# A two-layer cross-attention kernel with expert feed-forwards: gates spread by fp32r matmuls instead of through memory, and the second layer's first keys and queries loaded another way

## The chip, the core and the metric

The kernel runs on one core of a Trainium2 chip. The core has a matmul engine (TensorE, PE in the profile; PEld is its weight loads), a vector engine (DVE), a scalar engine (ACT), GpSimd (POOL) and SyncE (SP), which here issues nearly all DMAs. The engines run their own instruction streams and wait for each other by semaphores. The metric is the device time of one execution in microseconds (us). Before the change it is 2705.45 us, the median of three runs (2705.42 to 2705.73).

## The reference

Two layers work on x (1024 rows, 128 channels) against a context of 6404 rows. Each layer is a 16-head cross-attention (8 channels a head) and a feed-forward with 8 experts of which each row uses two, both added to x through a tanh gate.

```
def _L1_ffn_ref(x, W1, b1, W2, b2, Wr, br):
    logits = xf @ Wr + br
    topk_val, topk_idx = jax.lax.top_k(logits, K)          # K = 2 of 8 experts
    scores = jax.nn.softmax(topk_val, axis=-1)
    h = jnp.einsum('nd,edh->enh', xf, W1) + b1[:, None, :]
    a, g = jnp.split(h, 2, axis=-1)
    act = jax.nn.silu(a) * g
    out_e = jnp.einsum('enh,ehd->end', act, W2) + b2[:, None, :]
...
x = x + jnp.tanh(g_xattn[0]) * _L0_xattn_ref(_layernorm(x, axis=-1), ctx_1024, ctx_1024, ...)
x = x + jnp.tanh(g_ffn[0]) * _L0_ffn_ref(_layernorm(x, axis=-1), ...)
x = x + jnp.tanh(g_xattn[1]) * _L1_xattn_ref(ctx_1024, ctx_1024, _layernorm(x, axis=-1), mask, ...)
x = x + jnp.tanh(g_ffn[1]) * _L1_ffn_ref(_layernorm(x, axis=-1), ...)
```

Layer 0's experts have 512 hidden channels and a gelu; layer 1's have 256 hidden channels, a silu and a second product. The kernel computes all eight experts for all rows and multiplies each expert's hidden values by the row's gate, which is zero for the six experts that were not chosen.

## The kernel before

**Attention.** Keys and queries are projected for all heads at once, split into a high fp32r part and the remaining low part (`split_keys`, `queries`, L620), and stored to memory as `k_parts` and `q_parts` (`store_k` L255, `store_q` L261). For each head SP loads the 8 rows of that head back in the layout that the score matmuls need: `load_keys` (L297) issues 16 DMAs a head into one of the two slots of `k_ring`, and `load_queries` (L306) issues 4 into one of the three slots of `q_ring`. Each slot holds both parts twice, for two halves of the rows of x (partition rows 0 and 64). For each head PE first computes all scores once for the maxima (L947), DVE reduces them (L657), then PE computes them again (L928), ACT takes the exponentials (L495), and PE weighs the values (L976). The first head's maxima (`FIRST_UNITS`, 52 units of one L947 pair and one L657) stand alone at the start of each attention; later maxima are interleaved with the scores.

**Feed-forward.** `top_two` on DVE computes the gates `ga[:, 4]` (last instruction L782). PE turns them (`turn_gates`, L1056), ACT copies them out as `gate_t`, 8 partitions of 1024 (`gates_turned`, L518). Every engine below needs the gate of an expert on all 128 partitions. So `spread_gates` on SP (L351, L354) stores `gate_t` to memory as `gate_rows` and loads each of the eight rows back, broadcast to 128 partitions, as `gate_bc`, which lies in `k_ring`. `experts` on PE walks 16 units u = 0 to 15 (expert u // 2, half u % 2): `up(u)` is four matmuls (L1074), `down(u - 1)` is four in layer 0 and two in layer 1 (L1082). ACT applies gelu or silu (L528, L540). DVE multiplies the hidden values by the gate (L792 in layer 0; L805 and then L811 in layer 1), and `down` waits for that product.

**The hand-over between the layers.** Since `gate_bc` has overwritten `k_ring`, POOL must write the rows of ones again (`set_ring(1)`, L402, two memsets) after the last gate product of layer 0. SP, whose DMAs are issued in program order, then does `load_first(1)`: keys of head 0, the stores of the new queries (`store_q`), queries of heads 0 and 1, keys of head 1, queries of head 2. Meanwhile DVE, ACT and PE compute the layer norm and the queries of layer 1 (L604 to L620, L897, L905). PE's first maximum of layer 1 waits for the keys and the queries of head 0; ahead of it PE, DVE and SP each branch on a flag (L1122, L826, L276) between a masked and an unmasked program.

**The start.** SP stores the queries and the keys of layer 0, then does `load_first(0)`, and then loads the mask in ten pieces (`check_mask`, L267), which ACT sums (L467) in turn with its copies of the values (L440).

## Time and profile before

| What | us |
|---|---|
| median of three runs | 2705.45 |
| the profiled execution, its own time | 2710.2 |
| its span | 2708.1 |
| PE busy, DVE busy, ACT busy | 2494.6, 2161.4, 1939.4 |
| mean granted clock of PE | 0.941 |
| hidden-layer stages: layer 0, layer 1 (start of the gates to the last `down`) | about 1289 to 1416, 2598 to 2700 |
| hand-over between the layers, last `down` to the first maximum of layer 1 | about 1416 to 1466 |

The span is the profiled execution from the first to the last instruction; 2.1 us of its time lie outside the span, and the execution was 4.75 us above the median. The times in the rows below are microseconds from the start of the span. A granted clock of 1.00 is TensorE's level of 2.4 GHz, 0.50 its level of 1.2 GHz.

### The profile page before, as it was taken

How to read it: one execution, taken by the hardware profiler on the slowest of the kernel's cores; microseconds unless marked ns; L12 is line 12 of the kernel's file. 1: busy time of each engine (PE TensorE's matmuls, PEld its weight loads, DVE VectorE, ACT ScalarE, POOL GpSimd, SP SyncE). 2: the span in 40 equal slices, each digit the busy share in tenths (PEclk: the TensorE clock that was granted, in tenths of full speed). 3: DMA queues.
4: the chain of work that ended last, by engine and by line, in shares of the span. 5: the costliest groups of instructions: out<-in, count | busy, mean ns of one | idle time of the engine just before them, and what ended most of it. 6: DMA issues, size and time to landing. Idle time of an engine off the chain costs nothing.

```text
span 2708.1 us, 51412 instructions
## 1 busy us (share of the span) xinstructions
PE 2494.6 (92%) x21338; PEld 967.9 (36%) x21340; DVE 2161.4 (80%) x2211; ACT 1939.4 (72%) x3545; POOL 41.2 (2%) x28
## 2 busy tenths in 40 slices
PE   2389999999999999997893899999999999999979
PEld 1243333333333333343441333333333333333334
DVE  5468999999999999944434899999999999999234
ACT  2058888888888888874330188888888888888932
POOL 4000000000000000000010000000000000000000
PEclk8559999999999999999895699999999999999989
DMA  7120000000000000003101000000000000000010
GB/s 251 68 78 23 29 29 29 27 28 28 29 29 29 28 28 28 20 32 113 63 0 61 11 27 28 29 29 29 29 28 28 28 29 29 29 29 14 2 63 8
DMA packets 38612, 102.86 MB, mean 38 GB/s; under 512 B 4164, under 2 KB 14936, under 8 KB 38120
## 3 DMA queue, kind: packets, MB, share of 16 engines
q1 hardware_dynamic: 36936, 99.14, 10.0%
q8 instruction: 170, 2.79, 0.4%
q10 hardware_dynamic: 1440, 0.40, 0.1%
q14 instruction: 66, 0.54, 0.1%
HBM read 83.72 MB, written 15.80 MB: 37 GB/s over the span
## 4 chain that ended last, share of the span: by engine, by line
PE 64%; DVE 29%; SPq 3%; DMA 3%; issue 1%; ACT 1%; POOL 1%; ACTq 0%; DVEq 0%; POOLq 0%
DVE m_part L657 26%; PE ps L976 23%; PE ps L928 19%; PE ps L947 10%; PE ps L1074 4%; PE ps L1082 3%; SPq L297 2%; PE ps L888 1%; DMA q_parts<-probs 1%; PE ps L918 1%; SPq L306 1%; DMA probs<-in_mask_t 1%; PE ps L880 1%; PE ps L995 1%; DVE probs L613 1%
## 5 line engine op out<-in xcount | busy, mean ns | idle before, releaser
L657 DVE TENSOR_REDUCE m_part<-ps 128x2 f32<-128x1024 f32 (+1 forms) x1664 | 1933.7, 1184 | 209.0 <-PE ps L947 199.7
L495 ACT ACTIVATE probs<-ps 128x512 f32<-128x512 f32 (+1 forms) x3264 | 1763.8, 595 | 325.2 <-PE ps L928 213.6
L976 PE MATMUL ps<-probs,v_all 128*9 128x256 f32 x13056 | 1014.2, 383 | 1.7 <-ACT o_raw L475 0.5
L928 PE MATMUL ps<-q_ring,k_ring 35*128 35x512 f32 x3264 | 871.1, 498 | 0.6 <-ACT q_ring L484 0.4
L947 PE MATMUL ps<-k_ring,q_ring 33*128 33x512 f32 (+1 forms) x3328 | 733.7, 420 | 94.6 <-DVE m_part L657 36.2
L928 PEld LDWEIGHTS ps<-q_ring,k_ring 35*128 35x128 f32 x3264 | 349.5, 183 | 697.2 <-ACT probs L495 603.3
L947 PEld LDWEIGHTS ps<-k_ring,q_ring 33*128 33x128 f32 x3328 | 350.9, 194 | 183.2 <-DVE m_part L657 110.1
L976 PEld LDWEIGHTS ps<-probs,v_all 128*9 128x9 f32 x13056 | 195.3, 89 | 551.4 <-ACT probs L495 466.0
L792 DVE TENSOR_TENSOR probs<-probs,k_ring 128x512 f32<-128x512 f32 x64 | 43.6, 691 | 64.9 <-ACT probs L528 56.6
L678 DVE RECIPROCAL r_den<-ps 128x8 f32<-128x8 f32 x32 | 6.6, 207 | 110.6 <-PE ps L955 110.6
L482 ACT ACTIVATE q_ring<-ps 3x512 fp32r<-3x512 f32 x32 | 18.8, 587 | 102.2 <-PE ps L918 101.5
L528 ACT ACTIVATE probs<-ps,b_col 128x512 f32<-128x512 f32 x64 | 43.7, 687 | 65.5 <-PE ps L1074 58.5
L888 PE MATMUL ps<-w_att,ctx_t 128*128 128x128 f32 (+1 forms) x204 | 40.2, 358 | 31.7 <-ACT v_all L440 31.7
L467 ACT ACTIVATE probs<-probs 128x2560 bf16<-128x2560 uint16 (+1 forms) x11 | 23.9, 2177 | 60.2 <-DMA probs<-in_mask_t 60.1
L540 ACT ACTIVATE probs<-ps,b_col 128x512 f32<-128x512 f32 x32 | 20.2, 683 | 65.2 <-PE ps L1074 65.2
L1074 PE MATMUL ps<-big,ctx_t 128*128 128x512 f32 x128 | 61.3, 622 | 5.8 <-DVE probs L805 5.8
L1082 PE MATMUL ps<-probs,big 128*128 128x512 f32 x128 | 59.2, 608 | 4.5 <-DVE probs L792 4.5
L897 PE MATMUL ps<-ident_f,probs 128*128 128x128 f32 x32 | 8.8, 450 | 56.1 <-DVE probs L613 40.2
L1074 PE MATMUL ps<-big 128*128 128x512 f32 x128 | 59.2, 606 | 0.0
L402 POOL MEMSET k_ring<- 32x13056 f32 (+1 forms) x4 | 35.8, 8944 | 1381.9 <-DVE probs L792 1381.8
L805 DVE SCALAR_TENSOR_TENSOR probs<-ps,b_col,probs 128x512 f32<-128x512 f32 x32 | 23.9, 748 | 35.3 <-PE ps L1074 35.3
L888 PEld LDWEIGHTS ps<-w_att,ctx_t 128*128 128x128 f32 (+1 forms) x204 | 35.7, 256 | 43.4 <-ACT v_all L440 32.7
(122 smaller groups left out, 598.3 us busy)
## 6 DMA issues: line engine op xcount, KB each, us to landing
k_ring<-k_parts SPq DMA_DIRECT2D x384, 96.0 KB
k_ring<-k_parts SPq DMA_DIRECT2D x128, 112.2 KB
k_ring<-gate_rows SPq DMA_DIRECT2D x16, 512.0 KB, 7.3
probs<-in_mask_t SPq DMA_DIRECT2D x10, 640.0 KB, 4.4
k_parts<-probs SPq DMA_DIRECT2D x12, 512.0 KB, 3.1
k_parts<-big SPq DMA_DIRECT2D x12, 512.0 KB, 3.1
q_ring<-q_parts SPq DMA_DIRECT2D x128, 32.0 KB
big<-in_w SPq DMA_DIRECT2D x1, 2048.0 KB, 10.7
```

What stands on the lines that cost most here:

```text
L297: sp.dma_start(k_ring[row:row + PARTS * HD, off + k0:off + k1].bitcast(F32), of.broadcast_to([PARTS, HD, k1 - k0])).then_inc(key_in(l, h, ...
L402: nc.gpsimd.memset(k_ring[row:row + 32, 0:wide].bitcast(F32), 1.0).then_inc(sem("ring_set"), 1)
L495: A(probs[0:k, n % PSLOTS, HALF * half:HALF * half + HALF], ps[0:k, e_bank(unit), :], ACT.Exp, scale=SCALE).then_inc(sem(f"exp_done{l}"), 1)
L528: A(h_ring[:, u % 4, :], ps[:, u % 4, :], ACT.Gelu_apprx_tanh, bias=b1_col[:, 0, e * 4 + t:e * 4 + t + 1]).then_inc(sem("act_done0"), 1)
L657: V.tensor_reduce(m_part[:, h % 2, :, p, c], mx(n % 2)[:, :, 0:chunk_w[c]], AX.X, ALU.max).then_inc(sem(f"mx_done{l}"), 1)
L792: V.tensor_tensor(hg_ring[:, u % 8, :], h_ring[:, u % 4, :], gate_bc[:, e, HALF * half:HALF * half + HALF], ALU.mult).then_inc(sem("gated0 ...
L888: mm = pe.matmul(ps[0:width(t), bank + c % banks, P * (t % 4):P * (t % 4) + P], ctx_t[:, P * t:P * t + width(t)], w_att[:, l, 2, :], start ...
L928: pe.matmul(bank, k_ring[row:row + ROWS_EXP, koff:koff + P], q_ring[row:row + ROWS_EXP, qoff:qoff + HALF], start=not masked, stop=True).th ...
L947: mm = pe.matmul(bank[:, 0:w], q_ring[row:row + ROWS_MAX, qoff:qoff + P], k_ring[row:row + ROWS_MAX, koff:koff + w], start=not masked, sto ...
L976: mm = pe.matmul(ps[32 * g:32 * g + VW, 7, 0:QGW], v_all[:, t, h, :], probs[:, n % PSLOTS, QGW * g:QGW * g + QGW], start=(t == 0), stop=(t ...
L1074: pe.matmul(ps[:, t, :], w1[:, e, P * t:P * t + P], x_t[:, HALF * half:HALF * half + HALF], start=True, stop=True).then_inc(sem(f"hidden{l ...
L1082: mm = pe.matmul(ps[:, 4 + half, :], w2[:, e, t, :], hg_ring[:, n % 8, :], start=(e == 0 and t == 0), stop=False)
```

## The change

Three things change.

1. The gates no longer go through memory. DVE splits them into a high fp32r part and the rest (`gate_hl`, two instructions more), PE turns 16 rows in place of 8, ACT copies them to `gate_t`, which now lies in rows 0 to 15 of `q_ring`. For each unit u a matmul `spread(u)` with the constant `pick_e` (16 rows, each column repeated 128 times) writes the gate of the unit's expert and half, on all 128 partitions, to PSUM bank 6 or 7. DVE's products L792 and L811 (now L794 and L813) read the gate from there. The final matmul with b2 has 16 rows.
2. `k_ring` is not overwritten by gates, so the second pair of memsets on POOL is gone, and SP loads the keys of heads 0 and 1 of layer 1 as soon as they are stored and the last two heads of layer 0 are scored.
3. The first head's queries are copied from `q_st` straight into `q_ring`, by eight DMAs of 8 partitions each, ahead of the stores of the queries, in both layers. In layer 0 these now come before the stores of the keys.

```diff
-        gate_rows = [nc.dram_tensor(f"gate_rows{l}", [E, TQ], F32, kind="Internal").ap() for l in range(2)]
...
-        gate_bc = k_ring[:, 0:E * TQ].bitcast(F32).rearrange("p (e q) -> p e q", e=E)
...
                 for of in (flat3(probs)[:, 2 * TQ:], spare)]
-        gate_t = spare[0:E, KST * PARTS * HALF:KST * PARTS * HALF + TQ]
...
-        b2_sb = sb("b2_sb", [E, 2, C])
+        b2_sb = sb("b2_sb", [2 * E, 2, C])
+        pick_e = sb("pick_e", [2 * E, E], F32R)
...
+        gate_hl = spare[:, ga_at + 6 * QT * E + 6 * QT:ga_at + 8 * QT * E + 6 * QT].rearrange("p (t e) -> p t e", t=QT)
...
                                      ).then_inc(query_in(l, h)[0], 16)
-            def ready(l, what):
-
-                if what == "q":
-                    sp.wait_ge(sem(f"q_stored{l}"), 16 * 2)
-                else:
-                    for n in range(KST):
-                        sp.wait_ge(sem(f"k_stored{l}_{n}"), 16 * len(range(n, NCH, KST)))
-
-            def load_first(l):
-
-                sp.wait_ge(sem("ring_set"), RING_SET[l])
-                ready(l, "k")
-                if l:
+            def keys_stored(l):
+                for n in range(KST):
+                    sp.wait_ge(sem(f"k_stored{l}_{n}"), 16 * len(range(n, NCH, KST)))
+
+            def first_queries(l):
+
+                for half in range(2):
+                    sp.wait_ge(sem(f"q_split{l}"), half + 1)
+                    for b in range(PARTS):
+                        for part in range(PARTS):
+                            row = HB * half + (b * PARTS + part) * HD
+                            sp.dma_start(q_ring[row:row + HD, 0:HALF].bitcast(F32), q_st[0:HD, half, part, :].bitcast(F32)
+                                         ).then_inc(query_in(l, 0)[0], 16)
+                store_q(l)
+
+            def load_first0():
+
+                sp.wait_ge(sem("ring_set"), RING_SET)
+                first_queries(0)
+                store_k(0)
+                keys_stored(0)
+                for g in range(len(K_GROUPS)):
+                    load_keys(0, 0, g)
+                sp.wait_ge(sem("q_stored0"), 16 * 2)
+                load_queries(0, 1)
+                for g in range(len(K_GROUPS)):
+                    load_keys(0, 1, g)
+                load_queries(0, 2)
+
+            def load_first1():
+
+                keys_stored(1)
+                for h in range(KRING):
+                    sp.wait_ge(sem("scored0"), SCORE_AT["score", H - KRING + h, 2 * NT - 1] + 1)
                     for g in range(len(K_GROUPS)):
-                        load_keys(l, 0, g)
-                    store_q(l)
-                ready(l, "q")
-                load_queries(l, 0)
-                if l == 0:
-                    for g in range(len(K_GROUPS)):
-                        load_keys(l, 0, g)
-                load_queries(l, 1)
-                for g in range(len(K_GROUPS)):
-                    load_keys(l, 1, g)
-                load_queries(l, 2)
+                        load_keys(1, h, g)
+                first_queries(1)
+                sp.wait_ge(sem("q_stored1"), 16 * 2)
+                load_queries(1, 1)
+                load_queries(1, 2)
             def load_heads(l):
...
-            def spread_gates(l):
-                sp.wait_ge(sem(f"gate_t{l}"), 1)
-                sp.dma_start(gate_rows[l], gate_t[:, :]).then_inc(sem(f"gate_out{l}"), 16)
-                sp.wait_ge(sem(f"gate_out{l}"), 16)
-                for e in range(E):
-                    sp.dma_start(gate_bc[:, e, :], gate_rows[l][e:e + 1, :].rearrange("e q -> (e q)").partition_broadcast(P)
-                                 ).then_inc(sem(f"gate_bc_{e}"), 16)
-
...
             sp.dma_start(w2_1.rearrange("p e t d -> p (e t) d"),
                          a["w2_1"].rearrange("e (t f) d -> f (e t) d", f=P)).then_inc(sem("experts_in1"), 16)
-            spread_gates(0)
-            load_first(1)
+            load_first1()
             build_mask()
             load_heads(1)
-            spread_gates(1)
             sp.wait_ge(sem("x_final"), 1)
             sp.dma_start(out.rearrange("(t p) c -> p t c", p=P), x_sb[:, :, :]).then_inc(sem("out_stored"), 16)
...
+                nc.gpsimd.tensor_tensor(pick_e[:, :], ident_f[0:2 * E, 0:E], ident_f[0:2 * E, E:2 * E], ALU.add).then_inc(sem("pick_e"), 1)
...
-            set_ring(1)
...
-                A(gate_t[:, :], flat(ps[0:E, 6:8, :]), ACT.Identity).then_inc(sem(f"gate_t{l}"), 1)
+                A(gate_t[:, :], flat(ps[0:2 * E, 6:8, :]), ACT.Identity).then_inc(sem(f"gate_t{l}"), 1)
...
-                V.tensor_tensor(gate, tmp, spread(1), ALU.mult).then_inc(sem(f"gates{l}"), 1)
+                link(V.tensor_tensor(gate, tmp, spread(1), ALU.mult))
+                link(V.tensor_copy(gate_hl[:, :, 0:E].bitcast(F32R), gate))
+                V.tensor_tensor(gate_hl[:, :, E:2 * E], gate, gate_hl[:, :, 0:E], ALU.subtract).then_inc(sem(f"gates{l}"), 1)
             def gate_experts0():
                 for u in range(E * 2 * 4):
-                    e, half = u // 8, (u // 4) % 2
+                    half = (u // 4) % 2
                     dve.wait_ge(sem("act_done0"), u + 1)
-                    if u % 8 == 0:
-                        dve.wait_ge(sem(f"gate_bc_{e}"), 16)
+                    if u % 4 == 0:
+                        dve.wait_ge(sem("gate_spread0"), u // 4 + 1)
                     if u >= 8:
                         dve.wait_ge(sem("down0"), u - 7)
-                    V.tensor_tensor(hg_ring[:, u % 8, :], h_ring[:, u % 4, :], gate_bc[:, e, HALF * half:HALF * half + HALF],
+                    V.tensor_tensor(hg_ring[:, u % 8, :], h_ring[:, u % 4, :], ps[:, 6 + half, :],
                                     ALU.mult).then_inc(sem("gated0"), 1)
             def gate_experts1():
                                                scalar=b1_col[:, 1, e * 4 + 2 + t:e * 4 + 3 + t], in1=h_ring[:, slot, :],
                                                op0=ALU.add, op1=ALU.mult).then_inc(sem("glu1"), 1)
                         dve.wait_ge(sem("glu1"), n + 1)
-                        if half == 0 and t == 0:
-                            dve.wait_ge(sem(f"gate_bc_{e}"), 32)
-                        V.tensor_tensor(hg_ring[:, n % 8, :], hg_ring[:, n % 8, :], gate_bc[:, e, HALF * half:HALF * half + HALF],
+                        if t == 0:
+                            dve.wait_ge(sem("gate_spread1"), u + 1)
+                        V.tensor_tensor(hg_ring[:, n % 8, :], hg_ring[:, n % 8, :], ps[:, 6 + half, :],
                                         ALU.mult).then_inc(sem("gated1"), 1)
...
-                    mm = pe.transpose(ps[0:E, 6 + t // 4, P * (t % 4):P * (t % 4) + P], ga[:, 4, t, :], ident_f[:, :])
+                    mm = pe.transpose(ps[0:2 * E, 6 + t // 4, P * (t % 4):P * (t % 4) + P], gate_hl[:, t, :], ident_f[:, :])
                 mm.then_inc(sem(f"gate_turned{l}"), 1)
...
+                def spread(u):
+
+                    e, half = u // 2, u % 2
+                    if u < 2:
+                        pe.wait_ge(sem("pick_e"), 1)
+                        pe.wait_ge(sem(f"gate_t{l}"), 1)
+                    else:
+                        pe.wait_ge(sem(f"gated{l}"), nd * (u - 1))
+                    pe.matmul(ps[:, 6 + half, :], pick_e[:, e:e + 1].broadcast_to([2 * E, P]),
+                              gate_t[:, HALF * half:HALF * half + HALF], start=True, stop=True
+                              ).then_inc(sem(f"gate_spread{l}"), 1)
+
                 for u in range(2 * E):
                     up(u)
                     if u == 0:
                         turn_gates(l)
+                        spread(0)
                     if u:
+                        spread(u)
                         down(u - 1)
                 down(2 * E - 1)
                 pe.wait_ge(sem(f"gate_t{l}"), 1)
                 for half in range(2):
-                    mm = pe.matmul(ps[:, 4 + half, :], b2_sb[:, l, :], gate_t[:, HALF * half:HALF * half + HALF],
+                    mm = pe.matmul(ps[:, 4 + half, :], b2_sb[:, l, :], gate_t[:, HALF * half:HALF * half + HALF].bitcast(F32),
                                    start=False, stop=True)
                     mm.then_inc(sem(f"y_sum{l}"), 1)
```

On SP, from the last keys of layer 1 stored to the flag (k_parts, q_parts are in memory, `big` holds the keys' staging and the gates), before:

```order
L255 DMA k_parts<-big 256x1x260
L367 DMA ctx_t<-in_w_1 128x8x512
L368 DMA ctx_t<-in_w_1 128x16x128
L351 DMA gate_rows<-big 8x1024
L354 DMA k_ring<-gate_rows 128x1024 x8
L297 DMA k_ring<-k_parts 16x1x1536 x12
L297 DMA k_ring<-k_parts 16x1x1796 x4
L261 DMA q_parts<-probs 256x1x512 x2
L306 DMA q_ring<-q_parts 16x1x512 x8
L297 DMA k_ring<-k_parts 16x1x1536 x12
L297 DMA k_ring<-k_parts 16x1x1796 x4
L306 DMA q_ring<-q_parts 16x1x512 x4
```

The same place on SP now:

```order
L257 DMA k_parts<-big 256x1x260
L374 DMA ctx_t<-in_w_1 128x8x512
L375 DMA ctx_t<-in_w_1 128x16x128
L299 DMA k_ring<-k_parts 16x1x1536 x12
L299 DMA k_ring<-k_parts 16x1x1796 x4
L299 DMA k_ring<-k_parts 16x1x1536 x12
L299 DMA k_ring<-k_parts 16x1x1796 x4
L323 DMA q_ring<-probs 8x512 x8
L263 DMA q_parts<-probs 256x1x512 x2
L308 DMA q_ring<-q_parts 16x1x512 x8
```

The nine DMAs of the gates are gone, both heads' keys stand directly behind the expert weights, and eight small copies stand ahead of the stores of the queries.

On PE, the first units of layer 0's experts (`big` holds weights, rows and gates; `probs` the gated hidden values), before:

```order
L1074 MATMUL ps<-big 128x512 x4
L1056 MATMUL ps<-ident_f,big 8x128 x8
L1074 MATMUL ps<-big 128x512 x4
L1082 MATMUL ps<-probs,big 128x512 x4
L1074 MATMUL ps<-big 128x512 x4
```

The same place on PE now:

```order
L1076 MATMUL ps<-big 128x512 x4
L1058 MATMUL ps<-ident_f,big 16x128 x8
L1096 MATMUL ps<-q_ring,pick_e 128x512
L1076 MATMUL ps<-big 128x512 x4
L1096 MATMUL ps<-q_ring,pick_e 128x512
L1084 MATMUL ps<-probs,big 128x512 x4
L1076 MATMUL ps<-big 128x512 x4
```

One matmul L1096 is added behind the turned gates and one behind each later `up(u)`; the first of them stands ahead of `up(1)`, which before followed the turned gates directly.

On SP at the start of the program (`probs` holds the staging of queries and keys), before:

```order
L249 DMA big<-in_w_0 128x32x128
L261 DMA q_parts<-probs 256x1x512 x2
L255 DMA k_parts<-probs 256x1x512 x12
L255 DMA k_parts<-probs 256x1x260
L306 DMA q_ring<-q_parts 16x1x512 x4
L297 DMA k_ring<-k_parts 16x1x1536 x12
```

and now:

```order
L251 DMA big<-in_w_0 128x32x128
L323 DMA q_ring<-probs 8x512 x8
L263 DMA q_parts<-probs 256x1x512 x2
L257 DMA k_parts<-probs 256x1x512 x12
L257 DMA k_parts<-probs 256x1x260
L299 DMA k_ring<-k_parts 16x1x1536 x12
```

Eight small copies moved ahead of all stores, and the four loads of head 0's queries left the place between the stores and the first keys.

## Rows read from the trace of the kernel before

**Rows 1.** Chain of waits, whole run: start us, length us, what.
```profile
1310.81 5.40 PE ps L1082 x8
...
1410.48 6.93 POOL k_ring L402
...
1439.50 21.28 DMA q_parts<-probs
```

**Rows 2.** Timeline, hand-over: start us, us, engine line op [idle before <-releaser].
```profile
1267.01 0.80 SPq L368 DMA_DIRECT2D ctx_t<-in_w  x1
...
1424.40 13.47 SPq L297 DMA_DIRECT2D k_ring<-k_parts  x16
...
1431.75 0.75 DVE L620 SCALAR_TENSOR_TENSOR probs<-ps,b_col,probs 128x512 fp32r<-128x512 f32 x1 [0.85 <-ACT probs L459]
1437.91 4.79 SPq L261 DMA_DIRECT2D q_parts<-probs  x2
1460.80 5.04 SPq L306 DMA_DIRECT2D q_ring<-q_parts  x8
...
1465.98 1.22 PE L947 MATMUL ps<-k_ring,q_ring 33*128 33x512 f32 x4 [34.99 <-DMA q_ring<-q_parts]
1466.89 34.03 DVE L657 TENSOR_REDUCE m_part<-ps 128x2 f32<-128x1024 f32 x30 [34.39 <-PE ps L947]
```

**Rows 3.** Timeline, start of layer 0's experts.
```profile
1301.83 1.04 PE L1056 MATMUL ps<-ident_f,big 128*8 128x128 f32 x8 [2.05 <-DVE big L782]
...
1302.90 1.01 ACT L518 ACTIVATE big<-ps 8x1024 f32<-8x1024 f32 x1 [2.40 <-PE ps L1056]
1303.94 0.32 SPq L351 DMA_DIRECT2D gate_rows<-big  x1
...
1305.75 4.28 SPq L354 DMA_DIRECT2D k_ring<-gate_rows  x8
1316.04 3.60 PE L1074 MATMUL ps<-big 128*128 128x512 f32 x8
```

**Rows 4.** Timeline, start of layer 1's experts.
```profile
2610.08 0.22 DVE L782 TENSOR_TENSOR big<-big 128x64 f32<-128x64 f32 x1
...
2625.07 3.81 PE L1074 MATMUL ps<-big,ctx_t 128*128 128x512 f32 x8
```

**Rows 5.** Busy time in stretches: start:end, us; PE, PEld, DVE, ACT, POOL; PEclk, DMA share, GB/s.
```profile
40.00:57.00 17.00, 9.89 (x16) 2.91 (x16) 7.25 (x10) 6.02 (x10) 0.00 (x0) 0.85 0.86 326
...
1300.00:1303.00 3.00, 1.17 (x9) 0.92 (x10) 1.53 (x8) 0.60 (x2) 0.00 (x0) 1.00 0.00 0
1316.00:1416.00 100.00, 100.00 (x234) 44.28 (x233) 38.74 (x56) 38.47 (x56) 5.52 (x1) 1.00 0.03 10
...
1450.00:1460.00 10.00, 0.00 (x0) 0.00 (x0) 0.00 (x0) 0.00 (x0) 0.00 (x0) 0.50 0.13 52
```

**Rows 6.** Timeline of PE, fp32r (L947) and bf16 (L990) matmuls at the full clock.
```profile
190.75 0.49 PE L947 MATMUL ps<-k_ring,q_ring 33*128 33x512 f32 x2
191.18 1.25 PE L990 MATMUL ps<-probs,neg_i 128*128 128x512 bf16 x5
```

**Rows 7.** Timeline, end of layer 0's experts.
```profile
1408.74 7.03 PE L1082 MATMUL ps<-probs,big 128*128 128x512 f32 x16
...
1415.70 1.98 PE L1095 MATMUL ps<-big,b_sb 8*128 8x512 f32 x4
```

**Rows 8.** Timeline of the start, SP and ACT.
```profile
33.35 1.30 SPq L261 DMA_DIRECT2D q_parts<-probs  x2
34.99 20.32 SPq L255 DMA_DIRECT2D k_parts<-probs  x13
57.36 2.64 SPq L306 DMA_DIRECT2D q_ring<-q_parts  x4
...
134.01 2.34 ACT L467 ACTIVATE probs<-probs 128x2560 bf16<-128x2560 uint16 x1 [56.02 <-DMA probs<-in_mask_t]
```

**Rows 9.** DMA queues from 1433 to 1434: kind, packets, MB, share.
```profile
q8 instruction: 1, 0.02, 7.7%
```

More of the change, by code:

```diff
@@ L387, in link, with set_ring @@
                 pool.wait_ge(sem("pool_chain"), chain[0])
-            def set_ring(l):
-                wide = E * TQ if l else KRING * KW
-                if l:
-                    pool.wait_ge(sem("gated0"), 2 * E * 4)
-                cleared = []
-                if l == 0:
-                    cleared += [k_ring[row:row + 32, off + TK:off + KW] for row in (0, HB) for off in range(0, KRING * KW, KW)]
-                    cleared += [q_ring[row:row + 32, :] for row in (KR, HB + KR)]
+            def set_ring():
+                cleared = [k_ring[row:row + 32, off + TK:off + KW] for row in (0, HB) for off in range(0, KRING * KW, KW)]
+                cleared += [q_ring[row:row + 32, :] for row in (KR, HB + KR)]
                 for n, part in enumerate(cleared):
```

21 lines of the change are left out of this document (11 added, 10 removed).

## The prediction

> **What bounds the kernel now.** I read the chain of waits first, because the engines' shares alone (PE 92% busy) hide that PE stands still in a few places. In the chain the reader sees the two attentions as DVE and PE work that the change does not touch, and between them a piece in which no engine computes: POOL's memsets of `k_ring`, then one store of the queries whose landing takes 21.28 us [rows 1]. The timeline of that stretch gives the sizes: the low halves of the new queries are ready at 1431.75 + 0.75 = 1432.50, PE's first maximum starts at 1465.98 after 34.99 us of idling, and in between SP works off keys, stores and queries in the order in which they were written [rows 2]. The two stretches at the start of the experts are the second kind: PE and DVE wait for gates that make a round trip through memory [rows 3, 4]. The third place is the start of the kernel, where SP's order decides when the mask arrives, for which ACT waits 56.02 us [rows 8].
>
> **The hand-over, the large term.** The keys leave the critical place. They need both heads' DMAs, 2 x 16 of 96 to 112 KB, 3.3 MB in all, which run at 52 GB/s on 0.13 of 16 DMA engines [rows 5]: 63 us. SP can issue them as soon as layer 0 is scored and the expert weights are issued, behind L368 at 1267.8 [rows 2]; with 3.1 MB of weights ahead (10 us at the 326 GB/s that the stores reach [rows 5]) they have landed by about 1341, 90 us before they are needed. What is late next is the first head's queries. Their first half is ready at 1431.75 - 0.85 = 1430.90, the second at 1432.50. Each half is four copies of 8 partitions. An issue costs 0.32 us where 8 partitions go out (the gates' store) [rows 3] and 0.63 us where queries go in (5.04 for eight) [rows 2]; I take the middle, 0.47. Then the first four end at 1432.8, the last one is issued at 1434.2. From issue to landing the gates' 32 KB took 1.81 us (1303.94 to 1305.75) [rows 3]; the queries' loads took 5.18 from the first issue to PE's start [rows 2], less three issues of 0.63 is 3.3. That gives 1436.0 to 1437.5, and I take 1436.5; with cheap issues and the short landing it is 1435.3, with the dear ones and the long landing 1438.5. So the first maximum starts 1465.98 - 1436.5 = **29.5 us earlier** (27.5 to 30.7). It is not given back: the next 52 units are paced by DVE (34.03 us for 30 units, 1.13 each) [rows 2], whatever PE's clock is; the second head's keys are already there, and its queries, whose stores and loads follow the copies on SP, have 52 x 1.13 = 59 us. Behind the copies on SP only these and the flag are queued.
>
> By the Trainium skill ("DMA: Bandwidth & Descriptors", section "Why a DMA increments its semaphore by 16 and not by 1") the number of DMA engines that share a copy is the largest number up to 16 that divides the slowest dimension on both sides. The trace agrees for the keys (slowest dimension 2, share 0.13 = 2 of 16) [rows 5]. The eight copies of 8 partitions would by it use eight engines each; the 128 KB at the keys' 52 GB/s would need 2.5 us in all, by the rule a fourth of it, and both are below the 3.8 us of issues, so the sum stays.
>
> **Layer 0's experts, start.** Removed: the store, its landing and the eight broadcasts. Before, the gates are done at 1301.8, `up(1)` runs meanwhile, `down(0)` starts at 1310.81 and takes 5.40 in place of 3.43 because the clock has dropped during the wait, and `up(2)` starts at 1316.04 [rows 1, 3]. Now: two more DVE instructions of 64 columns (0.22 each plus the link, together 0.5 [rows 4]), so the turn starts at 1302.3; ACT's copy follows 1.07 later and takes 1.01 [rows 3], 16 partitions at the price of 8; `spread(0)` at 1304.4. Then 0.3 for it, 3.43 for `up(1)`, 0.3 for `spread(1)`, 3.43 for `down(0)`: `up(2)` starts at 1311.9, **4.1 us earlier**, if the clock holds. DVE's four products of unit 0 need 2.8 us beside `up(1)`.
>
> **What a spread costs.** In steady state PE is busy 100.00 of 100 us while DVE works 38.74 [rows 5], so each added matmul is paid in full, and a slower read from PSUM on DVE is covered. DVE now starts on unit u only after `spread(u)`, about 2 us later than before, but `down(u)` follows a whole `down` and `up` (6.9 us) later. Two fp32r matmuls of 512 columns take 191.18 - 190.75 = 0.43, so 0.22 each; a bf16 one takes 0.25 [rows 6]. A change from 128 rows to few costs about 0.1: sixteen matmuls of 0.429 from 1408.74 end at 1415.60, the next starts at 1415.70 [rows 7]. Lower bound 0.22, upper bound half an fp32 matmul plus the change, 0.53. I take 0.30, nearest to the fp32r row. Units 2 to 15: 14 x 0.30 = **+4.2 us** (3.1 to 7.4). Layer 0's experts thus come out at +0.1.
>
> **Layer 1's experts.** Gates done at 2610.30 + 0.5 [rows 4]; turn, copy and waits 2.25 as above: `spread(0)` at 2613.1; then 0.3, `up(1)` 3.43, 0.3, `down(0)` 1.72: `up(2)` at 2618.9 in place of 2625.07 [rows 4], **6.2 us earlier**. `up(1)`'s fourth matmul needs DVE's second product, which now waits only for `spread(0)`. Spreads 2 to 14 cost 13 x 0.30 = **+3.9**; the fifteenth is hidden, since the last `down` waits for DVE anyway. Sum -2.3.
>
> **The start.** Eight copies go ahead of the stores: at 0.47 they push the stores from 33.35 back by 3.8 us. The stores keep the DMA engines at 0.86 [rows 5], so little is caught up; say 3.2 stay. In return the four query loads (2.64 us of issuing [rows 8]) no longer stand ahead of the first keys, nor in the queue that then drains at the keys' rate up to the mask. Net between -2 and +2, and up to +4.7 if each copy costs 0.63 and the queue gives nothing back; I take 0. Two small loads of b2 are issued while SP would wait for the queries.
>
> **The sum.** -29.5 + 0.1 - 2.3 + 0 = -31.7 us. The gone memsets and the extra pick matrix on POOL lie beside other work. On the profiled execution: span 2708.1 to 2676.4, time 2710.2 to 2678.5. That execution was 4.75 above the median, so against the median 2705.45 - 31.7 = 2673.75; I forecast **2674**.
>
> **Rivals.**
> - *The spreads cost double.* If a single fp32r matmul with 16 rows takes the upper bound of 0.53, 27 of them cost 6.2 more: 2680. For it: nothing in the trace shows one alone, without a partner on the other half of the rows; against it, the pair's 0.43 [rows 6].
> - *A branch takes the place of the wait.* Ahead of the first maximum PE branches over the masked program. Before, that lay inside 34.99 us. An instruction packet moves between 1433 and 1434 [rows 9], which fits a fetch that PE or DVE needed; the new wait ends at 1436.5, so only some 3 us are left above it. If instructions are there only at 1441, the time is 2678.5. The Trainium skill ("Runtime: NRT & Kernel Launch", section "Instruction fetch mechanics") says that a taken branch out of the window stalls for a fetch; the packet agrees, no row shows its end.
> - *The start pays.* The stores move by the full 4.7 us and the queue gives nothing back: 2678.5.
> - *Slower: the experts lose the clock.* In 1300 to 1303 PE idles 2.05 us and keeps 1.00 [rows 3, 5]; now it idles 2.5 and 1.1 us around the turn and sixteen narrow matmuls are mixed in. If the granted clock stayed at 0.50 through layer 0's stage, its 100 us at 1.00 [rows 5] would become 200: 2774. It turns the sign from 32 us of that stage on. Against it: PE is without a gap there.
> - *It does not do what it says.* If the keys had not landed by 1436 the old wait would return, up to the whole 29.5: 2703. Against it stand the 90 us of margin.
>
> **How the numbers follow.** Forecast as worked out (2668.5 to 2677.5) 0.69; double spreads 0.10; branch 0.07; start 0.07; keys late 0.03; slower 0.04. The range takes the forecast and most of the first three rivals: 2668.5 to 2682. A change under 0.2% (5.4 us) cannot be told from none: faster 0.94, same 0.02, slower 0.04.
>
> **What would show it.** The first L947 of layer 1 about 4 us after the end of the last L620, waiting for the query copies; keys moving from about 1278 to 1341; PE starts L1076 of unit 1 about 2.4 us after the last gate instruction with the clock at 1.00; a period of 7.2 us a unit in layer 0 (6.87 before). Wrong would be a first maximum that waits for keys or for nothing visible, a unit longer than 7.4, or ACT's first mask sum later than 138.

## The result and the profile after

The change makes the kernel faster by less than forecast: a median of **2686.64 us** (2683.34 to 2688.53, four runs) against 2705.59 of before, ratio **0.9925** (95% interval 0.9911 to 0.9939). The forecast was 2674, with a range of 2668.5 to 2682. The profiled execution of after spans 2685.4 us and took 2687.49.

The chain of waits of after, by engine, has no POOL in it any more (L949, L1076 and L1084 are what L947, L1074 and L1082 were before):

```profile
PE 65%; DVE 29%; SPq 2%; DMA 1%; issue 1%; ACT 1%; ACTq 0%; DVEq 0%
```

**The hand-over**, timeline of after; it answers to [rows 2]:

```profile
1438.09 1.54 DVE L620 SCALAR_TENSOR_TENSOR probs<-ps,b_col,probs 128x512 fp32r<-128x512 f32 x2 [2.93 <-ACT probs L459]
...
1438.87 5.39 SPq L323 DMA_DIRECT2D q_ring<-probs  x8
1444.30 1.25 SPq L263 DMA_DIRECT2D q_parts<-probs  x2
...
1445.63 1.22 PE L949 MATMUL ps<-k_ring,q_ring 33*128 33x512 f32 x4 [7.52 <-DMA q_ring<-probs]
```

Its end in the chain of waits (start us, length us, what):

```profile
1442.96 0.62 SPq L323
...
1443.63 1.96 DMA q_ring<-probs
```

PE's 34.99 us of idling have become 7.52. The reader is to see what bounds them: eight issues of 0.67 us each on SP, which begin when the first L620 has ended (1438.86), then the last copy's landing, until 1445.63.

**The start of the experts**, layer 0 and layer 1, timeline of after (PE); it answers to [rows 3, 4]:

```profile
1305.47 1.04 PE L1058 MATMUL ps<-ident_f,big 128*16 128x128 f32 x8 [1.04 <-DVE big L784]
1307.71 0.47 PE L1096 MATMUL ps<-q_ring,pick_e 16*128 16x512 f32 x1 [1.19 <-ACT q_ring L518]
1308.10 3.70 PE L1076 MATMUL ps<-big 128*128 128x512 f32 x8
1311.73 0.50 PE L1096 MATMUL ps<-q_ring,pick_e 16*128 16x512 f32 x1
1312.16 3.70 PE L1084 MATMUL ps<-probs,big 128*128 128x512 f32 x8
1315.70 3.60 PE L1076 MATMUL ps<-big 128*128 128x512 f32 x8
1319.22 0.49 PE L1096 MATMUL ps<-q_ring,pick_e 16*128 16x512 f32 x1
...
2588.19 0.47 PE L1096 MATMUL ps<-q_ring,pick_e 16*128 16x512 f32 x1 [1.19 <-ACT q_ring L518]
...
2592.22 0.50 PE L1096 MATMUL ps<-q_ring,pick_e 16*128 16x512 f32 x1
...
2594.46 3.60 PE L1076 MATMUL ps<-big,ctx_t 128*128 128x512 f32 x8
2597.99 0.49 PE L1096 MATMUL ps<-q_ring,pick_e 16*128 16x512 f32 x1
```

From spread to spread are 1319.22 - 1311.73 = 7.49 us, where a unit took 6.87 before (16 matmuls of 0.43): **0.62 us a spread**, not 0.30. The same in layer 1: 5.77 (2597.99 - 2592.22) for 5.15.

**The start of the kernel**, timeline of after (SP, ACT); it answers to [rows 8]:

```profile
33.64 5.50 SPq L323 DMA_DIRECT2D q_ring<-probs  x8
39.19 1.28 SPq L263 DMA_DIRECT2D q_parts<-probs  x2
40.52 20.92 SPq L257 DMA_DIRECT2D k_parts<-probs  x13
...
118.54 21.45 SPq L269 DMA_DIRECT2D probs<-in_mask_t  x3
137.16 2.34 ACT L467 ACTIVATE probs<-probs 128x2560 bf16<-128x2560 uint16 x1 [56.56 <-DMA probs<-in_mask_t]
```

The stores start 5.84 us later than before (39.19 for 33.35), and ACT gets the mask 3.15 us later (137.16 for 134.01).

**Where the time went.** Executions of one kernel differ here by up to 13 us (those of e9b by 38), so I compare stages and not totals; executions more than 1.5% above their kernel's fastest (2722 to 4361 us) are left out of every median, and where one of them was the profiled one (e6, e7, e8b, e10b), I read from it only stretches in which PE's clock was that of the other kernels. A part of the difference is that PE's granted clock, after it has risen in an attention, falls once more for a few microseconds. The stretch in question in the two profiled executions:

```profile
1545.00:1550.00 5.00, 5.00 (x48) 2.02 (x44) 1.92 (x3) 1.64 (x4) 0.00 (x0) 0.50 0.00 0
```
```profile
1540.00:1550.00 10.00, 10.00 (x99) 3.57 (x99) 9.94 (x9) 8.86 (x17) 0.00 (x0) 1.00 0.07 29
```

The first is before (clock 0.50), the second after (1.00). Stages of the profiled executions, in us (attention 0 of e8b is left out, since its clock stayed at 0.50 until about 320). "First maximum" is the start of its first weight load. "Experts" run from the last `o_raw` of a layer to the b2 matmul and hold the gates; "hand-over" runs from there to the first maximum of layer 1:

| | before | before_again | after | after_again2 | e1 | e2 | e3 | e4 | e8b | e9b | e11 |
|---|---|---|---|---|---|---|---|---|---|---|---|
| first maximum, layer 0 | 71.22 | 71.17 | 73.82 | 73.80 | 71.15 | 73.78 | 73.87 | 73.90 | 73.88 | 71.03 | 71.04 |
| attention 0 | 1192.8 | 1191.0 | 1193.1 | 1192.9 | 1189.3 | 1189.7 | 1189.5 | 1189.6 | | 1189.4 | 1193.1 |
| experts 0 | 151.71 | 151.43 | 157.08 | 160.19 | 156.72 | 160.50 | 152.61 | 156.75 | 150.97 | 150.68 | 152.44 |
| hand-over | 50.29 | 50.26 | 21.60 | 21.85 | 21.76 | 21.77 | 21.39 | 20.05 | 21.77 | 21.88 | 20.05 |
| attention 1 | 1120.0 | 1118.7 | 1116.7 | 1119.4 | 1116.4 | 1116.0 | 1120.6 | 1120.4 | 1117.2 | 1117.8 | 1116.9 |
| experts 1 | 113.82 | 112.38 | 114.72 | 115.98 | 114.75 | 118.41 | 111.08 | 114.73 | 110.35 | 109.06 | 109.04 |

After against before: +3.0 at the start (2.6 of it at the first maximum), +5.4 in experts 0, -28.7 in the hand-over, -3.3 in attention 1 (the clock of this one execution of before), +0.9 in experts 1 (+2.35 against before_again, since before had the clock down for a piece of it): -22.7 in all, the difference of the two spans. Without the clock's part it is -18; the medians say -19. After_again2's experts 0 took 3.1 us more than after's: PE's clock fell to 0.50 at the end of the wait for the gates (PE idle for 2.66 and 1.19 us in it, in after for 1.04 and 1.19), and `up(1)` took 6.59 us in place of 3.70:

```profile
1308.03 6.59 PE L1076 MATMUL ps<-big 128*128 128x512 f32 x8
```

From `up(2)` to the b2 matmul no such fall disturbs the numbers: this piece takes 108.33 and 82.63 us in after (layer 0 and 1), 99.66 and 74.59 in before_again, 111.60 and 85.86 in e2, 102.93 and 77.54 in e8b. So the 14 and 13 added spreads cost 0.62 each.

### The profile page after: what moved, and what is told of

Read it like the earlier page. It is cut to its first block, busy times and chain, and to the rows that moved or that the text cites. A ratio compares the mean times of both kernels' runs of the same rounds, so it can differ in the third digit from the quotient of the medians.

```text
span 2685.4 us, 51482 instructions
## 1 busy us (share of the span) xinstructions
PE 2506.9 (93%) x21370; PEld 966.6 (36%) x21372; DVE 2157.0 (80%) x2215; ACT 1939.5 (72%) x3545; POOL 27.6 (1%) x27
## 4 chain that ended last, share of the span: by engine, by line
PE 65%; DVE 29%; SPq 2%; DMA 1%; issue 1%; ACT 1%; ACTq 0%; DVEq 0%
DVE m_part L657 26%; PE ps L978 23%; PE ps L930 19%; PE ps L949 10%; PE ps L1076 4%; PE ps L1084 3%; SPq L299 1%; PE ps L890 1%; PE ps L920 1%; DMA probs<-in_mask_t 1%; PE ps L882 1%; PE ps L997 1%; DVE probs L613 1%; PE ps L992 1%; SPq L308 1%
## 5 line engine op out<-in xcount | busy, mean ns | idle before, releaser
L949 PE MATMUL ps<-k_ring,q_ring 33*128 33x512 f32 (+1 forms) x3328 | 732.9, 420 | 63.5 <-DVE m_part L657 36.2
L949 PEld LDWEIGHTS ps<-k_ring,q_ring 33*128 33x128 f32 x3328 | 350.0, 194 | 152.0 <-DVE m_part L657 109.2
L794 DVE TENSOR_TENSOR probs<-probs,ps 128x512 f32<-128x512 f32 x64 | 39.7, 683 | 74.5 <-ACT probs L528 70.1
L1076 PE MATMUL ps<-big 128*128 128x512 f32 x128 | 60.8, 620 | 0.0
L1076 PE MATMUL ps<-big,ctx_t 128*128 128x512 f32 x128 | 60.1, 614 | 0.0
L1084 PE MATMUL ps<-probs,big 128*128 128x512 f32 x128 | 58.9, 604 | 0.0
L636 DVE TENSOR_SCALAR big<-ps,b_col 128x512 fp32r<-128x512 f32 (+1 forms) x13 | 9.5, 730 | 50.5 <-PE ps L882 50.5
```

The source lines that it names most:

```text
L794: V.tensor_tensor(hg_ring[:, u % 8, :], h_ring[:, u % 4, :], ps[:, 6 + half, :], ALU.mult).then_inc(sem("gated0"), 1)
L949: mm = pe.matmul(bank[:, 0:w], q_ring[row:row + ROWS_MAX, qoff:qoff + P], k_ring[row:row + ROWS_MAX, koff:koff + w], start=not masked, sto ...
L1076: pe.matmul(ps[:, t, :], w1[:, e, P * t:P * t + P], x_t[:, HALF * half:HALF * half + HALF], start=True, stop=True).then_inc(sem(f"hidden{l ...
L1084: mm = pe.matmul(ps[:, 4 + half, :], w2[:, e, t, :], hg_ring[:, n % 8, :], start=(e == 0 and t == 0), stop=False)
```

## The experiments

The letters S, P and W name edits that the combined kernels take over.

**before_again.** The kernel before, unchanged.

> The kernel before, once more, with a profile. In the profiled execution of before PE's clock was at 0.50 between 1545 and 1550 us and the execution took 2710.2 us, where the median of its others is 2705.45. First theory: that stretch of low clock belongs to single executions and not to the kernel; then another profile shows, if it has no such stretch, about 2705.5 us and 4 to 5 us less between the first maximum of layer 1 (L620) and the last attention output. Second theory: it belongs to the kernel's timing in that place; then every profile of it shows the low clock there and some 2710 us with the profiler, and the change really gained 3.3 us there.

2706.89 us median of ten, 2705.21 with the profile. The low clock is there again, a few microseconds earlier and 1.3 us cheaper. So neither theory holds as it was put: the stretch came in both profiled executions of before, in varying size. Kernels with one and the same attention 1 took 1116.0 to 1120.6 in it (table), so I don't count its 3.3 us as won by the change.

**after_again2.** The changed kernel, unchanged.

> The changed kernel once more, beside the next three on one chip. Its profiled execution had 3.5 us more in the first attention than four other kernels with the same instructions there. Theory: that was a dip of the clock in one execution; here the first attention (first score matmul to last o_raw) takes 1189.6 us, and the time is between 2683.5 and 2688. Rival: it belongs to the kernel, and the stretch takes 1193.1 again.

2689.32 us (2683.24 to 2694.37, six runs); ratio 0.9929 (0.9911 to 0.9947), the same as the first measurement. Attention 0 took 1192.9, not 1189.6: a miss for the theory, and what its rival said. Against the rival, e2, e3 and e4 run the same instructions there in 1189.5 to 1189.7, and e11 needs 1193.1 where e9b and e1 need 1189.3 to 1189.4. No kernel was seen with both values, so whether it goes with the kernel or with the execution stays open. Before took 1192.8 and 1191.0 there, so the change is not charged with it.

**e1_start_old (S).** Layer 0's start in the old order:

```diff
+                store_q(0)
+                store_k(0)
                 sp.wait_ge(sem("ring_set"), RING_SET)
-                first_queries(0)
-                store_k(0)
                 keys_stored(0)
+                sp.wait_ge(sem("q_stored0"), 16 * 2)
+                load_queries(0, 0)
                 for g in range(len(K_GROUPS)):
                     load_keys(0, 0, g)
```

> The changed kernel with the start of layer 0 as it was: the queries go to memory and come back, and the keys follow. First theory: the new order of the start is what makes the first score matmul (L949) 2.6 us and everything in the first attention 2.96 us late; then this kernel has its first L949 at about 71.3 us, the first mask sum at about 134.0, and takes 3.0 us less than the changed kernel, about 2683.6. Rival: the start moves but the attention, which is paced by VectorE, takes it back before the experts of layer 0, or the 3 us come from something else that the change added (the constants' extra copies, the spread's selector); then the time is within 0.7 us of the changed kernel's.

First maximum at 71.15, first mask sum at 134.40:

```profile
134.40 2.34 ACT L468 ACTIVATE probs<-probs 128x2560 bf16<-128x2560 uint16 x1 [56.47 <-DMA probs<-in_mask_t]
```

Median 2680.34 us of 2680.16, 2680.34 and 2687.90; the lowest is 3.1 below the lowest of after (2683.24). The last `o_raw` of layer 0 stands 3.0 us earlier than in e2, e3 and e4, with an attention 0 of the same length. The first theory is right: the direct copy of layer 0's queries costs 2.7 to 3.0 us.

**e2_double.** Each spread twice:

```diff
+                    pe.matmul(ps[:, 6 + half, :], pick_e[:, e:e + 1].broadcast_to([2 * E, P]),
+                              gate_t[:, HALF * half:HALF * half + HALF], start=True, stop=True)
                     pe.matmul(ps[:, 6 + half, :], pick_e[:, e:e + 1].broadcast_to([2 * E, P]),
```

> The changed kernel with each of its 32 spread matmuls issued twice in a row (the same result twice); 27 of them stand on the path of the expert stages. First theory, a spread is expensive by itself: a lone fp32r matmul of 16 rows and 512 columns takes about 0.42 us of TensorE at full clock, and about 0.19 us of its 0.61 is the switch to it and back. The double then costs 0.42 more for each, about 11.5 us in all (2698.1), with a half-expert period of 7.90 us in layer 0 and 6.19 in layer 1. Rival, the matmul itself takes 0.21 as was forecast and 0.40 is waiting around it (switch, semaphore): 5.8 us more (2692.4), periods 7.69 and 5.98.

Timeline of PE:

```profile
1315.86 0.49 PE L1096 MATMUL ps<-q_ring,pick_e 16*128 16x512 f32 x1
1316.19 0.39 PE L1098 MATMUL ps<-q_ring,pick_e 16*128 16x512 f32 x1
1316.51 3.70 PE L1084 MATMUL ps<-probs,big 128*128 128x512 f32 x8
```

0.33 + 0.32 = 0.65 us from the first spread to the expert's matmul where one alone takes 0.42: the second costs 0.23. Experts 0 grew by 3.75 (16 x 0.23) over e4, experts 1 by 3.68. My first theory, that the matmul itself takes 0.42, falls; the rival (2692.4) holds, with a median of 2692.27. So the forecast's 0.22 for the matmul itself was right, and of the **0.39 us around it** the forecast had only 0.08.

**e3_paired (P).** The gates of half 1 in partitions 64 to 79, two spreads at once, one pair for each expert:

```diff
-        gate_t = q_ring[0:2 * E, 0:TQ]
+        gate_t = [q_ring[HB * half:HB * half + 2 * E, 0:HALF] for half in range(2)]
...
+                    for half in range(2):
+                        row = HB * half
+                        pe.matmul(ps[:, 6 + half, :], pick_e[row:row + 2 * E, e:e + 1].broadcast_to([2 * E, P]),
+                                  gate_t[half], start=True, stop=True).then_inc(sem(f"gate_spread{l}"), 1)
```

> The changed kernel with the gates of the second half of the tokens held in partitions 64 to 79, so that the two spreads of an expert stand in different row halves of TensorE and are issued as one pair, once for each expert instead of one for each half-expert. First theory: two fp32r matmuls in the two row halves run side by side, the pair takes about 0.43 us as pairs of L947 did, and the switch is paid once; a pair then costs about 0.61 as a single one did, so some 13 to 14 spreads of 0.61 go: 8 to 8.5 us less, about 2678.4. Rival, they don't run side by side (0.42 each in a row) and only the switch is saved: 13 x 0.19 = 2.5 us less, about 2684.1. Rival, the later start of a pair (it waits for both products of the expert before) becomes a wait of its own: no gain or a loss.

Timeline of PE:

```profile
1344.20 0.50 PE L1100 MATMUL ps<-q_ring,pick_e 16*128 16x512 f32 x2
1344.62 3.70 PE L1087 MATMUL ps<-probs,big 128*128 128x512 f32 x8
...
1358.55 0.50 PE L1100 MATMUL ps<-q_ring,pick_e 16*128 16x512 f32 x2
```

Both matmuls fit into the 0.42 of one; two units take 14.35 where four stages of 3.43 take 13.73, so a pair costs the 0.62 of a single one. Experts 0 and 1 came out 4.1 and 3.65 us shorter than in e4 (the turn as plain matmuls and two copies on ACT take back about 0.6). Median 2678.93 us, 2678.4 expected.

**e10b_fp32.** The spread as a plain fp32 matmul, still 16 rows (`.bitcast(F32)` on both operands).

> The changed kernel with the spread as a plain fp32 matmul, still of 16 rows. First theory (the number of rows makes the switch dear): the matmul itself goes from 0.21 to 0.43, the length that the fp32 matmuls of 512 columns beside it have, or 0.85 if it takes four passes, and the 0.40 of the switch stay: 0.83 or 1.25 for each, 6 or 17 us more in all (2692 or 2704). Rival (the type makes it dear): the 0.40 goes, so 0.43 or 0.85 for each: 5 us less or 6 us more (2681.5 or 2693); the trace tells, by whether the weight load of a spread starts beneath the matmul before it.

Timeline of PE:

```profile
1322.87 3.60 PE L1076 MATMUL ps<-big 128*128 128x512 f32 x8
1326.39 1.12 PE L1096 MATMUL ps<-q_ring,pick_e 16*128 16x512 f32 x2
1327.44 3.70 PE L1084 MATMUL ps<-probs,big 128*128 128x512 f32 x8
1330.98 3.60 PE L1076 MATMUL ps<-big 128*128 128x512 f32 x8
```

A unit takes 8.11, so a spread 1.24: the 0.86 of two matmuls at 0.43 plus 0.38. The fp32r type is gone, the 0.38 stays. Experts 1 grew by 10.0 over e4 (16 x 0.62). The lowest time is 2703.24, 20 above the lowest of after; the median is 2713.61.

**e8b_rows128 (W).** The spread over all 128 rows, zeros in the selector below row 16:

```diff
+        gate_all = q_ring[:, 0:TQ]
...
-        pick_e = sb("pick_e", [2 * E, E], F32R)
+        pick_e = sb("pick_e", [P, E], F32R)
...
-                    pe.matmul(ps[:, 6 + half, :], pick_e[:, e:e + 1].broadcast_to([2 * E, P]),
-                              gate_t[:, HALF * half:HALF * half + HALF], start=True, stop=True
+                    pe.matmul(ps[:, 6 + half, :], pick_e[:, e:e + 1].broadcast_to([P, P]),
+                              gate_all[:, HALF * half:HALF * half + HALF], start=True, stop=True
```

> The changed kernel with the spread matmul over 128 rows instead of 16: the selector has zeros in rows 16 to 127, and the moving side is the whole of q_ring, whose other rows hold old queries. First theory, the switch between matmuls of 128 rows and of 16 rows is what is dear: the weight load then doesn't start beneath the matmul before it, and 0.40 of a spread's 0.62 us is two uncovered loads of 0.107 and two gaps of 0.1. With 128 rows everywhere the load hides, a spread costs 0.22 to 0.25, and 27 of them give 10 to 10.8 us back: about 2676.2. Rival, the switch between fp32 and fp32r is what is dear: 0.62 as before, 2686.6, with the gaps of 0.09 to 0.1 around each spread unchanged. Between them: one of the two gaps goes.

PE's granted clock is 1.00 in the stretch shown. Timeline (PE and PEld) of e8b, then the same place of a unit in after:

```profile
2639.68 3.60 PE L1077 MATMUL ps<-big,ctx_t 128*128 128x512 f32 x8
...
2642.26 0.19 PEld L1077 LDWEIGHTS ps<-big,ctx_t 128*128 128x128 f32 x1 [0.24 <-issue]
2642.69 0.19 PEld L1097 LDWEIGHTS ps<-q_ring,pick_e 128*128 128x128 f32 x1 [0.24 <-issue]
2642.72 0.79 PE L1097 MATMUL ps<-q_ring,pick_e 128*128 128x512 f32 x1
...
2645.06 3.60 PE L1077 MATMUL ps<-big,ctx_t 128*128 128x512 f32 x8
```
```profile
1318.27 0.19 PEld L1076 LDWEIGHTS ps<-big 128*128 128x128 f32 x1 [0.24 <-issue]
...
1319.22 0.18 PEld L1096 LDWEIGHTS ps<-q_ring,pick_e 16*128 16x128 f32 x1 [0.76 <-issue]
1319.22 0.49 PE L1096 MATMUL ps<-q_ring,pick_e 16*128 16x512 f32 x1
...
1319.64 0.30 PEld L1084 LDWEIGHTS ps<-probs,big 128*128 128x128 f32 x2 [0.24 <-issue]
```

The reader is to see when the weights of a matmul load. With 128 rows everywhere a load starts one matmul (0.43) after the last one, beneath the running matmul: 2642.26, 2642.69. In after the last matmul ahead of the spread begins at 1318.70 (1315.70 + 7 x 0.43), but the spread's load does not start beneath it: it starts at 1319.22, when that matmul had ended at 1319.13 and 0.09 more had gone by. The change back is the same: a gap of 0.10, then an uncovered load, for the two loads of L1084 start 0.30 - 0.19 = 0.11 apart. So 0.62 = 0.09 + 0.11 + 0.21 (the matmul, half of an fp32 one) + 0.10 + 0.11. A unit in e8b takes 2645.06 - 2639.68 = 5.38 for 5.77, a spread 0.23. The first theory is right: **the change of the number of rows, not of the type, made it dear**. The median is 2678.3 us (lowest 2673.86, 9.4 below the lowest of after).

By the Trainium skill ("TensorEngine Tiling (Array Packing)", section "Key Properties") changing the tiling mode drains TensorE, and different tiles work in parallel. The trace agrees with both: the gaps of 0.09 and 0.10 where 128 rows and 16 meet, and e3's two spreads in the time of one. That rule spoke against the change and was not weighed in the prediction.

**e4_split.** Layer 1's eight direct copies on two queues:

```diff
-                    for b in range(PARTS):
+                    for b in range(PARTS - l):
...
+            for half in range(2):
+                act.wait_ge(sem("q_split1"), half + 1)
+                for part in range(PARTS):
+                    row = HB * half + (PARTS + part) * HD
+                    act.dma_start(q_ring[row:row + HD, 0:HALF].bitcast(F32), q_st[0:HD, half, part, :].bitcast(F32)
+                                  ).then_inc(sem("q_in_0"), 16)
```

> The changed kernel with the eight direct copies of layer 1's first queries issued on two queues, four by SyncE (heads' first part) and four by ScalarE (second part), instead of eight by SyncE. In the changed kernel SyncE spends 5.4 us on eight issues of 0.67 us. Theory, the issue bounds the copies: four issues are 2.7 us, so the first maximum of layer 1 (L620) comes about 2.7 us earlier after the last LayerNorm step, and the time is 2683.9. Rival, the queries are held by something later (the transfer's landing of 2 us, the last LayerNorm step): only the last copy of each half counts, 1 to 1.5 us. Rival, nothing is gained because ScalarE is busy there.

Timeline:

```profile
1435.38 3.42 ACTq L578 DMA_DIRECT2D q_ring<-probs  x4
...
1438.38 1.58 SPq L263 DMA_DIRECT2D q_parts<-probs  x2
...
1440.30 1.22 PE L955 MATMUL ps<-k_ring,q_ring 33*128 33x512 f32 x4 [4.96 <-DMA q_ring<-probs]
```

The hand-over is 20.05, 1.6 to 1.8 shorter than in the two profiles of after, not 2.7. The issues bound it, but ACT's first one waits behind ACT's own evacuation (L459, same start, 0.69 long) and the four end at 1438.80. Median 2685.94 us: 0.7 below after, less than executions of one kernel differ, so the gain is read from the stage alone.

**e7_keys_late.** Layer 1's keys loaded after the last gate product; the copies stay direct, the memset stays out:

```diff
-                for h in range(KRING):
-                    sp.wait_ge(sem("scored0"), SCORE_AT["score", H - KRING + h, 2 * NT - 1] + 1)
...
+                sp.wait_ge(sem("gated0"), 2 * E * 4)
+                for g in range(len(K_GROUPS)):
+                    load_keys(1, 0, g)
                 first_queries(1)
...
                 load_queries(1, 1)
+                for g in range(len(K_GROUPS)):
+                    load_keys(1, 1, g)
```

> The changed kernel with layer 1's keys loaded not under the feed-forward stage but after the last gate product of layer 0 (head 0's before the query copies, head 1's behind them); the queries are still copied directly and the memset is still gone. First theory: of the 28.7 us that the hand-over gave, the early keys are only a part of about 6 to 7 us, since 16 key loads of some 1.0 to 1.7 us of issue and landing now come before the query copies; the first maximum of layer 1 comes 6 to 7 us later, about 2693. Rival: the keys are most of the gain, and the time goes to about 2708 to 2715. Rival: the loads are hidden under the LayerNorm steps and the time stays within 1 us of 2686.6.

Timeline of SP and the chain behind it:

```profile
1415.94 14.46 SPq L299 DMA_DIRECT2D k_ring<-k_parts  x16
1435.25 5.39 SPq L323 DMA_DIRECT2D q_ring<-probs  x8
```
```profile
1440.02 11.86 DMA q_ring<-probs
...
1451.92 0.81 PE ps L951 x2
```

The median is 2696.25 us, 9.6 above after. The hand-over is 31.66: 9.9 to 10.1 us longer, more than my 6 to 7 and far from the 21 to 28 of the rival. The keys were issued by 1430.40 but had not drained (head 0's 1.6 MB need some 31 us at the keys' 52 GB/s, an estimate); the last query copy was issued behind them and landed after 11.86 us in place of 1.96. So of the 28.7 us some 10 are lost when the keys come late, and the other 19 stay with the direct copies and the dropped memset, which no run takes apart.

**e6_combined** (S, P and e4's edit) and **e9b_best** (S, W and e4's edit).

> The start of layer 0 in the old order, the spreads in pairs over the two row halves, and the first query copies of layer 1 on two queues, together. If the three terms are what the theory says (3.0, 8.2, 2.7 us) and stand in different places, they add up: 2686.6 less 13.9, about 2672.7. Rival: the pair saves only the switch (2.5), then about 2678.4.

> The start of layer 0 in the old order, the first query copies of layer 1 on two queues, and spreads of 128 rows, together. By the first theory 2686.6 less 3.0 (start), 1.6 (copies, as measured alone) and 10.4 (spreads) is 2671.6, 15 us below the changed kernel and 34 below the one before. By its rival (type) 2682.

e6: median 2676.76 us (lowest 2675.85), 4.1 above the expected sum. e9b: lowest 2670.01, median 2677.04 of six from there to 2708.52, a ratio with an interval of 0.9882 to 0.9970, too wide to tell. The stages of e9b show S and W at their full size (first maximum 71.03; experts 150.68 and 109.06, 6.0 and 5.7 less than in e1) and the copies' gain gone: 21.88. The place, in e9b:

```profile
1426.17 3.73 ACTq L580 DMA_DIRECT2D q_ring<-probs  x4
...
1429.00 1.42 SPq L264 DMA_DIRECT2D q_parts<-probs  x2
...
1432.98 1.22 PE L957 MATMUL ps<-k_ring,q_ring 33*128 33x512 f32 x4 [6.86 <-DMA q_ring<-probs]
```

ACT's last copy was issued at 1429.19, after SP's store had started at 1429.00; it took 3.75 us to land (3.80 in e6, also 0.19 us behind the store's start), in e4 2.09 with the store behind it.

**e11_final.** e9b, and SP waits for the copies before it stores:

```diff
+                if l:
+                    sp.wait_ge(*query_in(l, 0))
                 store_q(l)
```

> The combined kernel once more (old start, copies on two queues, spreads of 128 rows), and SyncE now waits for the eight copies to land before it starts the store of the queries. In the combined kernel the store's first issue (1429.00) came ahead of ScalarE's last copy (1429.19), and that copy landed 3.75 us after its issue where 2.09 was measured when the store came behind. First theory: the copy waits behind the store's descriptors; then it lands in about 2.1 us, the first maximum comes 1.7 us earlier (20 us after the last expert matmul, not 21.9), and the time is about 1.7 below the combined kernel's, with a lowest of some 2668.3. Rival: the 3.75 is a matter of the two queues themselves, and the time stays. The second head's queries are needed some 59 us after the first maximum, so their later store costs nothing.

```profile
1431.61 3.67 ACTq L582 DMA_DIRECT2D q_ring<-probs  x4
...
1436.64 1.27 SPq L264 DMA_DIRECT2D q_parts<-probs  x2
...
1436.66 1.22 PE L959 MATMUL ps<-k_ring,q_ring 33*128 33x512 f32 x4 [5.20 <-DMA q_ring<-probs]
```

The last copy lands 2.06 us after its issue and the hand-over is 20.05 again: the copy had been delayed by the store ahead of it, not by the two queues as such. **2670.88 us** (2670.36 to 2672.77, four runs; the rival of an unchanged time is out by the stage, and 2668.3 as the lowest was not reached), ratio to before 0.9862 (0.9842 to 0.9883): 37 us below before, 16 below the change as made.

## Why the prediction missed

- **What a spread costs: the step that failed.** 0.30 us was forecast, 0.62 measured, outside the bounds of 0.22 and 0.53. 27 spreads at 0.32 more are **8.6 of the 13.7 us** between the forecast -31.7 and the -18 of the stages; the rest is 3.0 at the start, 0.8 in the hand-over and 1.3 at the two starts of the experts. A unit took 7.49 us, which fires the prediction's own sign of being wrong (above 7.4). The matmul itself was sized right (0.22; e2: 0.23). The change of rows was seen in [rows 7] (0.1) and then charged once, within the 0.08 on top; it comes four times, as two gaps and two loads that nothing covers (e8b, e10b). The rows of [rows 7] held half of that: the gap of 0.10, and behind it four matmuls that take 1.98 in place of 3 x 0.43 + 0.59 = 1.88 (0.59 is what the last of a row of eight has, 3.60 - 7 x 0.43). Those of [rows 6] show two fp32r matmuls and 0.43 us to a matmul of 128 rows; I halved it as if they ran one after the other. By e3 a pair runs side by side, so that 0.43 can be read as one matmul's 0.21 with the load and the gap of the change. The rival of double spreads, at a chance of 0.10, came nearest, but by another mechanism: it let the matmul itself take half an fp32 matmul's time and the change come once.
- **The start.** 0 was forecast (-2 to +2, at most +4.7), +3.0 measured; e1 takes it back whole. The error is the issue: 0.69 us a copy (5.50 for eight), not 0.47, and of the 5.8 us only 2.7 came back, where the forecast let all of its 3.2 come back. The four query loads that are gone from ahead of the keys took 2.64 us [rows 8].
- **The hand-over.** -29.5 was forecast, -28.7 measured. The mechanism was right in each part: keys moved early (SP's queue runs at 52 to 56 GB/s until about 1340), PE waits for the query copies, nothing is given back. Two sizes erred, one against the other: with issues of 0.67 us in place of 0.47 the last one began 19.60 us after the b2 matmul and not 18.5, and it landed in 1.96 and not 2.3. The end of the last L620 does not matter: it stands 15.60 after the b2 matmul in after and 16.60 in e1, and the first maximum 21.60 and 21.76.
- **The start of the experts.** `up(2)` came 3.3 us earlier in layer 0 (4.1 forecast) and 5.7 in layer 1 (6.2 forecast; against before_again). Spreads 0 and 1 at their real price explain 0.6 in each. The rival that lost the clock for the whole stage is out, but its mechanism is there in small: the clock was kept through the wait in after and fell in after_again2, which cost 3.1 us. The forecast's "if the clock holds" is thus not met in every execution.
- **Branch and fetch.** No wait of that kind: the chain goes from the last issue over 1.96 us of landing to PE.
- **The range.** Its upper end of 2682.0 let in one rival at a time. The true prices of the spreads and of the start together bring the forecast to 2674 + 8.6 + 3.0 = 2685.6. The issue costs at the start and in the hand-over came from one number, 0.47, and erred together; in the hand-over a landing taken 0.3 us too long hid a part of it.

## What to carry to other kernels

A matmul of 16 rows between matmuls of 128 costs more here than its columns: price it by the distance of its neighbours' starts, and if the selector's other rows can be zeros, fill them (the moving side then needs finite numbers in those rows, here old queries). Terms that rest on the same unmeasured number err together, and the range must add them. When a transfer becomes the last thing waited for, count its issues, and look at what another queue puts in front of it.

## What the runs showed of the hardware

- PE at full clock: an fp32r matmul of 16 rows and 512 columns costs 0.62 us between matmuls of 128 rows (0.23 for a second one behind it, 0.62 for a pair in the two row halves), 0.23 with 128 rows, and as fp32 with 16 rows 1.24.
- An SBUF copy of 8 partitions, 16 KB, takes 0.62 to 0.69 us to issue on SP and 1.96 us from issue to landing; behind 16 key loads 11.86.
- A copy on ACT's queue landed 1.7 us later when a store of two times 512 KB on SP's queue was issued 0.19 us ahead of it (e9b against e11; the same delay in e6). By the Trainium skill ("DMA: Bandwidth & Descriptors", section "Queues, rings and completion order") each DMA engine takes the queues in turn, a packet at a time. The trace does not decide it: in e9b the copy landed at 1432.94, behind the store's first DMA (1432.54) and ahead of its second (1434.36).
- PE's granted clock falls from 1.00 to 0.50 once more for some microseconds soon after it has risen, in some profiles for longer than in others; in the 5 us in which the fall began PE was busy for 4.23 (before, 1540 to 1545; before_again, 1535 to 1540) and 4.22 (e3, 1510 to 1515); stages of the same instructions differ by up to 4.6 us (attention 0: 1189.2 to 1193.1; attention 1: 1116.0 to 1120.6). What decides it was not found.
